# Layer 1 of a two-layer transformer kernel: the products of values of two steps issued together, with exponentials kept for three steps

## The reference, cut to what matters

```python
# layer 1's attention
k = x @ Wk
v = x @ Wv
q = jnp.einsum('btc,qcd->bqtd', x, Wq)
wei = jnp.einsum('bqtd,bsd->bqts', q, k) * scale
wei = jnp.where(causal, wei, -jnp.inf)
wei = jax.nn.softmax(wei, axis=-1)
out = jnp.einsum('bqts,bsd->btqd', wei, v)
return out.reshape(b, t, -1) @ Wp + bp
```

## Time and profile before

| | us |
|---|---|
| median of 3 runs | 1082.84 (1081.09 to 1083.71) |
| the profiled execution's own time | 1081.7 |
| its span, first to last instruction | 1079.9 |
| PE busy | 1004.5 (93%) |
| DVE busy | 897.2 (83%) |
| ACT busy | 823.3 (76%) |
| POOL busy | 195.4 (18%) |

### The profile page before, as it was taken

The page is one execution under the profiler, slowest core; times in us unless marked ns, Lnnn a source line. Parts: engine busy times, 40 slices in busy tenths (PEclk is TensorE's granted clock), DMA queues, the critical chain, the costliest instruction groups (busy, mean ns, idle before and its releaser), DMA issues.

```text
span 1079.9 us, 22146 instructions
## 1 busy us (share of the span) xinstructions
PE 1004.5 (93%) x8642; PEld 340.9 (32%) x8642; DVE 897.2 (83%) x1138; ACT 823.3 (76%) x1582; POOL 195.4 (18%) x370
## 2 busy tenths in 40 slices
PE   3979999999999999999998999999989998899997
PEld 2332222222222222222222345433344563323323
DVE  5899999999999999999999877756778768897604
ACT  3229999998999998999987677676755676656785
POOL 4533200003000003000023200331042113110112
PEclk9569999999999999999999999999999999999997
DMA  3460520100000000000000541114200431200000
GB/s 110 114 169 6 129 50 8 25 2 2 2 2 2 2 2 2 2 2 2 2 2 9 171 129 47 40 42 91 29 1 10 144 104 37 34 10 1 1 11 11
DMA packets 47694, 42.07 MB, mean 39 GB/s; under 512 B 6534, under 2 KB 45798, under 8 KB 47590
## 3 DMA queue, kind: packets, MB, share of 16 engines
q1 hardware_dynamic: 45190, 35.17, 13.1%
q0 software_dynamic: 1824, 5.25, 1.7%
q10 hardware_dynamic: 576, 0.23, 0.1%
HBM read 26.83 MB, written 13.30 MB: 37 GB/s over the span
## 4 chain that ended last, share of the span: by engine, by line
PE 70%; DVE 12%; ACT 8%; issue 4%; SPq 2%; DMA 2%; POOL 1%; ACTq 0%; POOLq 0%; DVEq 0%
PE O L957 26%; PE T L925 14%; PE S L884 8%; DVE mx L1236 7%; PE S L891 5%; ACT PT L1482 4%; PE T L934 4%; PE S L1070 2%; PE S L1036 1%; SPq L1858 1%; ACT PT L1476 1%; PE S L1026 1%; PE T L1078 1%; PE T L966 1%; PE S L934 1%
## 5 line engine op out<-in xcount | busy, mean ns | idle before, releaser
L1236 DVE TENSOR_REDUCE mx<-S 128x2 f32<-128x1024 f32 (+2 forms) x672 | 759.1, 1181 | 74.4 <-PE S L884 29.3
L1482 ACT ACTIVATE PT<-T 128x512 f32<-128x512 f32 (+2 forms) x1280 | 675.7, 580 | 111.2 <-PE T L934 49.2
L957 PE MATMUL O<-PT,Va 128*9 128x256 f32 (+1 forms) x4032 | 316.4, 386 | 3.3 <-ACT Os L1517 3.3
L884 PE MATMUL S<-Ks,Qs 48*128 48x512 bf16 x1024 | 205.5, 394 | 15.1 <-DVE mx L1236 8.9
L925 PE MATMUL T<-Qs,Ks 51*128 51x512 bf16 x1024 | 201.4, 385 | 10.9 <-ACT PT L1482 6.6
L925 PEld LDWEIGHTS T<-Qs,Ks 51*128 51x128 bf16 x1024 | 56.2, 93 | 220.7 <-issue 126.3
L957 PEld LDWEIGHTS O<-PT,Va 128*9 128x9 f32 x4032 | 59.8, 88 | 206.1 <-issue 196.5
L891 PE MATMUL S<-K,Qs 96*128 96x512 bf16 (+3 forms) x320 | 89.8, 350 | 5.1 <-DVE mx L1236 4.7
L934 PE MATMUL T<-Qs,K 99*128 99x512 bf16 (+3 forms) x256 | 67.5, 345 | 11.5 <-ACT PT L1482 7.8
L957 PE MATMUL O<-PT,V 128*17 128x512 f32 (+3 forms) x616 | 73.1, 544 | 0.0
L884 PEld LDWEIGHTS S<-Ks,Qs 48*128 48x128 bf16 x1024 | 52.6, 95 | 38.2 <-DVE mx L1236 28.2
(11 more groups left out here) (295 smaller groups left out, 816.1 us busy)
## 6 DMA issues: line engine op xcount, KB each, us to landing
Qs<-in_L_ffn_experts SPq DMA_DIRECT2D x28, 192.0 KB, 2.6
Ks<-in_L_ffn_experts SPq DMA_DIRECT2D x20, 192.0 KB, 2.5
Vf<-sorted_x SPq DMA_DIRECT2D x12, 256.0 KB, 4.8
sorted_y<-Vf SPq DMA_DIRECT2D x12, 256.0 KB, 2.3
Qs<-rows_q SPq DMA_DIRECT2D x24, 128.0 KB, 4.5
rows_q<-q SPq DMA_DIRECT2D x7, 384.0 KB, 2.5
Qs<-rows_q SPq DMA_DIRECT2D x36, 64.0 KB
sorted_x<-XP POOLq DMA_DIRECT2D x1, 1792.0 KB, 10.7
```

What stands on the lines that cost most here:

```text
L884: m = e.matmul(two[:, i, :], Qs[r0:r0 + 48, hp, q0:q0 + 128], Ks[r0:r0 + 48, hp, CH * kb:CH * kb + CH], start=True, stop=True, tile_positi ...
L957: m = e.matmul(acc[32 * g:32 * g + d1, lo:hi], v, PT[(2 * j + g // 2) % 4][:, p0 + lo:p0 + hi], start=fresh, stop=True, skip_group_check=n ...
L1236: e.tensor_reduce(mx[:, u % 2, h0:h0 + 2, kb], two[:, :, 0:n], AX.X, ALU.max).then_inc(free, 1)
L1482: e.activation(PT[(2 * j + pair) % 4][:, CH * i + lo:CH * i + CH], bank[:, lo:CH], ACT.Exp).then_inc(free, 1)
```

## The change

Layer 1's products of values of an even step are held back and issued right before those of the odd step behind it, so two steps' products stand together after every second step's `st`. This holds for steps 256 to 331; the last four, 332 to 335, are issued one by one as before, and layer 0 is unchanged. Since the product of an even step now comes one step later, a step's exponentials must live for three steps: layer 1 has six buffers in place of four, and the two new ones lie in the memory of layer 0's value tiles. ACT's wait before an exponential becomes `J - 2` in layer 1, but never less than all steps of layer 0.

```diff
+    def emit_values(J):
+
+        if STEPS0 <= J < len(steps) - 4:
+            if J % 2:
+                emit_pv(J - 1, (0, 1))
+                emit_pv(J, (0, 1))
+        else:
+            emit_pv(J, (0, 1))
...
-            emit_pv(J - LAG, (0, 1))
+            emit_values(J - LAG)
...
+        Vaf = Va[:, :, :, :].rearrange("p t h d -> p (t h d)")
+        PT = [b[:, :] for b in PT] + [Vaf[:, 1024 * i:1024 * i + 1024] for i in range(2)]
...
+        def exps(L, j, pair):
+
+            return PT[(2 * j + pair) % (6 if L else 4)]
...
-                        m = e.matmul(acc[32 * g:32 * g + d1, lo:hi], v, PT[(2 * j + g // 2) % 4][:, p0 + lo:p0 + hi], start=fresh,
+                        m = e.matmul(acc[32 * g:32 * g + d1, lo:hi], v, exps(L, j, g // 2)[:, p0 + lo:p0 + hi], start=fresh,
...
-                        ac.wait_ge(pv_done, J - 1)
-                        both = PT[(2 * j + pair) % 4][:, :].rearrange("p (i n) -> p i n", i=2)[:, :, lo:CH]
+                        ac.wait_ge(pv_done, J - 2)
+                        both = exps(L, j, pair)[:, :].rearrange("p (i n) -> p i n", i=2)[:, :, lo:CH]
...
                         if J >= 2:
-                            ac.wait_ge(pv_done, J - 1)
-                        e.activation(PT[(2 * j + pair) % 4][:, CH * i + lo:CH * i + CH], bank[:, lo:CH], ACT.Exp).then_inc(free, 1)
+                            ac.wait_ge(pv_done, max(J - 2, min(J - 1, STEPS0)))
+                        e.activation(exps(L, j, pair)[:, CH * i + lo:CH * i + CH], bank[:, lo:CH], ACT.Exp).then_inc(free, 1)
...
-                    both = PT[(2 * j + pair) % 4][:, :].rearrange("p (i n) -> p i n", i=2)[:, :, lo:lo + 128]
+                    both = exps(L, j, pair)[:, :].rearrange("p (i n) -> p i n", i=2)[:, :, lo:lo + 128]
```

## The result

The changed kernel takes 1094.41 us, the median of four runs (1092.74 to 1097.76), against 1082.21 of the kernel before, run beside it (four runs, 1081.09 to 1083.71). The ratio is 1.0111, 95% interval 1.0096 to 1.0126: 12.0 us slower, give or take 1.6. The forecast was 1087.4 with a range to 1092. Direction right, size half, and the range missed.

The account below looks back on a forecast made before the run. PE was taken to bound most full stretches, DVE beside it with three score products, ACT the last unit; 4.6 + 2.1 + 0.3 - 1.3 = +5.7 on 1081.7 gave 1087.4 us, range 1083 to 1092.

Parts of the forecast that it names:

- Price of a product: Values products, layer 1: a pair passes both borders with the scores once, saves 0.21 us and takes 1.83.
- Last unit: Steps 320 to 331: ACT idles 1.10 us per pair where it idled 0.26; six pairs, sum +4.6 us.
- Three score products: Steps 290 to 301: DVE idles 0.7 us per pair, three pairs counted, +2.1 us, bounds 0 and 4.2.
- Two score products: Steps 302 to 315: the 0.21 us saved becomes a wait for a T bank; +0.3 us, bounds 0 and 1.
- Rest: Steps 256 to 267, 282 to 289, 316 to 319: end moves through DVE, POOL and transfers, or products are narrow; 0.
- Moved steps and waits: Whole change: no DMA or POOL work moves, ACT's looser wait and the third buffer cost nothing; 0.
- Experts' stretch: Steps 268 to 280 or so: PE full, ACT's banks free in time; six pairs at -0.21, -1.3 us.
- the bound of -3.4: Lower bound for the early steps: all sixteen pairs up to step 289 save 0.21 us each.
- case 3: Rival: bursts starve DVE wherever S banks are shared, early part included; +12.6 us, 1094.3, chance 0.1.

## Why the prediction was wrong

- **Price of a product, pair:** right. 1.85 for a forecast 1.83, and 0.87 for the second product, so the border's 0.21 is real in size. It paid nothing in any stretch of steady steps, since in each of them another engine had a bank to wait for.
- **Last unit, +4.6:** right in mechanism and size (4.6 in the profile, 4.2 alone). The count "banks in hand against the burst plus the way in and out" gave the period, 5.0 for a measured 5.02. The idle time in it is 1.25 for 1.10, and four exponentials take 3.77, not 3.89.
- **Three score products, +2.1:** right in mechanism and sum (2.5 in the profile, 2.2 in the trace and 3.1 give or take 1.0 by the medians of these pairs alone). The pieces differ: DVE idles 0.82 for a forecast 0.7, but it idled 0.29 before, where the forecast had "just hidden". The loss is 0.4 in each of five pairs, not 0.7 in three.
- **Two score products, +0.3:** the steady step is right (6.28 for 6.24), the stretch isn't. It ends beside feed-forward work, steps 314 to 319, of which the forecast counted the last four at 0 under "Rest"; alone the pairs gain 3.0, with those at the start 1.9, and 1.3 in both traces.
- **Moved steps and waits, 0:** right by the kernel without pairs, -0.3.
- **Experts' stretch, -1.3:** this step failed. "PE is full, and every step carries so much other PE work that ACT's banks are free in time" looked at T banks, and took PE's 39.44 of 40 as proof that nothing waits. It is proof that nothing waited with the products where they were. The experts' products share S banks with the score products that DVE reads; the product of values was the filler between two uses of one bank. Measured +2.9 alone, and +1.9 in the whole change's profile.
- **Rest, 0:** this step failed too: +2.2 at the start of the layer, +0.7 in steps 281 to 290, +3.0 at step 291 in the profile; the pairs of 282 to 291 alone cost 2.2 by their medians. "The end moves through DVE, POOL and transfers" was taken for indifference. Where the end passes between engines, a product that covered part of PE's wait for DVE is worth its time, and its going makes the wait longer, as at step 291, where that costs 0.4. The rest of the 3.0 there, and 1.3 at step 262, is the lower clock behind the wait, which made the mixing product take 1.91 for 1.02. It was in no case of the forecast, and it also comes without pairs.
- **A slip:** up to step 289 there are seventeen pairs, not sixteen; the bound of -3.4 becomes -3.6, and nothing else changes.

The likeliest case had its rival in case 3, bursts that starve DVE wherever S banks are shared, 1094.3 at a chance of 0.1. It came out, 0.1 us from the median, and so near by luck: its reason holds for the experts (+2, measured +1.9 to +2.9), but it gave the two-product stretch +1 where it gains, and knew nothing of the clock. What should have raised its chance was in the earlier trace rows: from 785 to 825 us PE had 35.62 of 40 and DVE 31.86, so neither was full there even before, and the clock of that window stood at 0.96.

## What to carry to other kernels

Before grouping work on an engine, compare the burst, with the way in and out, to what the other engines hold in filled banks, in every stretch of the program; and ask of each piece that you take away from a place what it covered there, since a full engine proves only that its present order has no holes. A reordering doesn't have to hold everywhere: the pairs in 302 to 319 alone make a kernel 0.28% faster (0.9972, interval 0.9959 to 0.9985) where all of them make it 1.1% slower. Where an engine waits a microsecond or two for another, look at the durations behind the wait too; in the changed kernel's profile 2.6 of the 3.0 us at step 291 were lost there. And before such a loss is put down to the change, look for the same place in a kernel without it.

## What was unexpected of the hardware

- TensorE's granted clock fell to 0.50 (1.2 GHz) for 3.4 or 6.8 us behind PE's waits of 1.3 to 2.1 us inside otherwise full work, but not each time. At step 291 the kernel without pairs waits 1.44, as the kernel before, and yet it has the lower clock there where the kernel before has 1.00:

```profile
932.95 1.04 PE L908 MATMUL S<-K,Qs 96*128 96x512 bf16 x2 [1.44 <-DVE mx L1253]
933.78 1.91 PE L1102 MATMUL T<-Ks,wkk 128*128 128x512 f32 x2
```

  This one lost 2.7 us on the kernel before between the starts of steps 291 and 293, so nearly all of the changed kernel's 3.0 at this place can come without any pair. At step 262 it is the other way round: the kernel before has 3.4 us of the lower clock, the one with pairs from step 302 on has none, behind the same wait of 1.86, and gains 1.1 us there. A cost of this kind is a chance in each execution. The 17 profiled executions suggest that a longer wait raises the chance. At steps 262 and 291, waits of 1.98 to 2.11 had the lower clock behind them in 10 of 12 cases, waits of 1.85 or 1.86 in 5 of 7, waits of 1.44 in 3 of 9, and waits of 1.23 or 1.31 in none of 3 (but the 1.30 at step 284 above had it). With so few cases, at two places of the program, this isn't settled.
- Two executions of the same code differ by 3 us before layer 1 begins, and the kernel before takes 1089.70 us on one chip and 1082.28 to 1083.18 on others. A profile of one execution has to be lined up at a common point before its stretches are compared.
